# Merging key blocks in a bank, a whole bias table with reversed queries, short last units and a hand-placed job table in a fused attention and expert layer

## The reference

```python
x = x + attn(layernorm(x))
#   Q, K, V = silu(x @ Wq), silu(x @ Wk), silu(x @ Wv);  U = x @ Wu
#   scores = (Q K^T + rel_bias[i - j + 255]) / sqrt(16), NEG where j > i or K's row is all zero
#   attn = (silu(scores) @ V) * silu(U)          (silu, not softmax)
x = x + ffn(layernorm(x))
#   logits = x @ w_gate.T; top 2 of 8, softmax over the two; y = sum_e gate_e * (x @ w_in[e].T) @ w_out[e].T
```

## Time and profile before

| what | value |
|---|---|
| median of 3 runs | 362.77 us (362.26 to 366.17) |
| profiled execution, its time | 364.07 us |
| its span | 360.8 us |
| mean granted TensorE clock | 0.92 |
| TensorE matmuls busy | 318.1 us |
| VectorE busy | 256.8 us |
| ScalarE busy | 235.4 us |
| GpSimd busy | 142.3 us |
| DMA, mean | 101 GB/s |

### The profile page before, as it was taken

The page is one execution under the profiler, slowest core; times in us unless marked ns, Lnnn a source line. Parts: engine busy times, 40 slices in busy tenths (PEclk is TensorE's granted clock), DMA queues, the critical chain, the costliest instruction groups (busy, mean ns, idle before and its releaser), DMA issues.

```text
span 360.8 us, 5741 instructions
## 1 busy us (share of the span) xinstructions
PE 318.1 (88%) x1728; PEld 137.7 (38%) x1728; DVE 256.8 (71%) x773; ACT 235.4 (65%) x485; POOL 142.3 (39%) x205
## 2 busy tenths in 40 slices
PE   4699975999999899899988999999999989998392
PEld 3442422555343343234323444443334423423240
DVE  3545671747749958676768978878789597786586
ACT  2345883889974776587745786788757885774022
POOL 3541120102108660138156551085286313654446
PEclk9998995999999987699989987999999998999678
DMA  6618968124924930005914940028449200010001
GB/s 207 174 48 208 194 179 247 58 60 121 236 54 146 224 70 2 1 8 171 214 16 143 221 105 0 0 70 224 89 144 222 73 2 0 1 31 1 0 9 49
DMA packets 30685, 36.31 MB, mean 101 GB/s; under 512 B 3256, under 2 KB 17080, under 8 KB 30656
## 3 DMA queue, kind: packets, MB, share of 16 engines
q1 hardware_dynamic: 30080, 35.69, 39.9%
q10 hardware_dynamic: 576, 0.26, 0.3%
HBM read 23.87 MB, written 12.08 MB: 100 GB/s over the span
## 4 chain that ended last, share of the span: by engine, by line
PE 50%; DVE 25%; ACT 9%; DMA 8%; issue 5%; SPq 2%; POOL 0%; DVEq 0%
PE jobp L637 12%; PE o_acc L568 12%; PE score L555 8%; DVE score L809 8%; ACT wts L696 7%; PE jobp L599 4%; DMA rows_dram<-k_hi 3%; DVE xn L853 3%; DVE ymix L922 3%; PE jobp L630 3%; PE jobp L657 2%; DMA rows_dram<-q_lo 2%; PE jobp L592 2%; DVE stats L840 2%; DMA ymix<-in_L_ffn_w_out 2%
## 5 line engine op out<-in xcount | busy, mean ns | idle before, releaser
L696 ACT ACTIVATE wts<-score,far 128x512 f32<-128x512 f32 (+3 forms) x384 | 193.4, 589 | 69.7 <-DVE score L809 57.9
L809 DVE TENSOR_TENSOR score<-score,bias_near 128x384 f32<-128x384 f32 (+2 forms) x320 | 119.0, 436 | 33.4 <-PE score L555 33.0
L507 POOL TENSOR_TENSOR ymix<-ymix 128x512 f32<-128x512 f32 (+2 forms) x84 | 69.4, 826 | 82.3 <-DVE ymix L922 77.9
L555 PE MATMUL score<-q_stack,k_stack 64*128 64x512 f32 (+3 forms) x352 | 82.1, 426 | 10.1 <-ACT wts L696 4.5
L568 PE MATMUL o_acc<-wts,v_pad 128*32 128x512 f32 (+3 forms) x768 | 86.8, 525 | 2.3 <-DVE oT L821 1.4
L555 PEld LDWEIGHTS score<-q_stack,k_stack 64*128 64x128 f32 x352 | 39.9, 193 | 74.9 <-issue 47.5
L637 PE MATMUL jobp<-mm_e,xn2T 128*128 128x512 f32 x116 | 65.5, 669 | 0.0
L922 DVE TENSOR_TENSOR ymix<-jobp,gates 128x512 f32<-128x512 f32 x56 | 38.0, 686 | 20.4 <-PE jobp L637 19.6
L637 PEld LDWEIGHTS jobp<-mm_e,xn2T 128*128 128x128 f32 x116 | 20.0, 201 | 31.9 <-issue 27.7
L455 POOL TENSOR_TENSOR rstd<-mv,eps_t 128x4 f32<-128x4 f32 x16 | 3.2, 201 | 69.3 <-DVE mv L843 69.3
L568 PEld LDWEIGHTS o_acc<-wts,v_pad 128*32 128x32 f32 x768 | 15.4, 109 | 26.5 <-issue 18.7
(11 more groups left out here) (92 smaller groups left out, 272.3 us busy)
## 6 DMA issues: line engine op xcount, KB each, us to landing
k_stack<-rows_dram SPq DMA_DIRECT2D x32, 256.0 KB, 5.7
q_stack<-rows_dram SPq DMA_DIRECT2D x28, 256.0 KB, 6.4
rows_dram<-k_hi SPq DMA_DIRECT2D x16, 256.0 KB
xs<-in_L_attn_x SPq DMA_DIRECT2D x8, 256.0 KB, 7.9
rows_dram<-k_lo SPq DMA_DIRECT2D x8, 256.0 KB
rows_dram<-q_hi SPq DMA_DIRECT2D x7, 256.0 KB
rows_dram<-q_lo SPq DMA_DIRECT2D x7, 256.0 KB
out<-xs SPq DMA_DIRECT2D x7, 256.0 KB, 2.3
```

The costliest lines, as they stand in the source:

```text
L507: then_wait(pool.tensor_tensor(y[:, 0:n], y[:, 0:n], y[:, n:2 * n], ALU.add))
L555: pe.matmul(score[bank][:, 0:n], keys, queries, start=True, stop=True).then_inc(scored[bank], 1)
L696: act.activation(wts[:, number % 2, j, 0:n], score[bank][:, 0:n], ACT.Silu, bias=far[:, h:h + 1], scale=HD ** -0.5).then_inc(weighed[bank], 1)
L809: dve.tensor_tensor(scores, scores, bias_near[:, 4 * quad + j, c0:c0 + near], ALU.add)\
```

## The change

- **Units and groups.** `UNITS` replaces the halves. The last half of the last batch becomes two units of two tiles. In a unit of four tiles the diagonal blocks of 384 and 128 queries form one group of 512 columns in one bank; in a unit of two tiles two key blocks of 256 queries do. A half 0 has 3 groups a quad, a half 1 has 7, the last units 3 and 4: 20 a batch, 80 in all. Each block is still its own score matmul, bias addition and P·V product; one activation covers the bank. There are 320 activations instead of 384.
- **Bias.** Queries lie reversed within a half: the Q product reads its rows backwards, and the gating reads `o_acc` backwards. The transfers from `bias_dram` then write the final table, and flip, FLIP jobs and their copies go. The table has 512 columns of whole bias (the first 128 filled with the far value by GpSimd). Groups that lie within it add all their columns and use no far value; others use `bias_rel` (the difference to far, made on GpSimd by `REL`: two subtractions of 1024 columns) and the far value as before.
- **Jobs.** `plan_timeline` goes; the table of slots is written out, with up to three banked jobs in a slot. Three slots precede group 0. T1, Q and K of half 1 of batch 0 stand beside groups 1 and 2, K of half 0 is split directly, and experts 1 and above follow from slot 6 on.
- **Norms.** All except norm1 of batch 0 and norm2 of the last unit run on GpSimd, behind their reciprocal root: 14 normalisations, 54 tiles.
- **Top 2.** An 8-wide maximum sorts a tile's logits; comparisons with its second entry choose, and gates take two operations.
- **Loads.** Expert 1 is loaded behind the write of `bias_dram`; experts 4 to 7 are issued from ScalarE's queue behind the `M` of the expert they replace. Rows of q and k of half 1 are written together. `kpad` lies in the place of batch 3's x.
- **End.** SEL to FF of two tiles only. Their four FF products wait in four score banks, and `MIX` adds expert by expert from PSUM on VectorE, two tiles in turn. The last two stores go from two queues.

```diff
+UNITS = [(b, HT * half, HT) for b in range(B - 1) for half in range(2)] + [(B - 1, 0, HT), (B - 1, HT, 2), (B - 1, HT + 2, 2)]
...
+def part(u, kb):
+    b, f, tiles = UNITS[u]
+    return u, kb, P * (f + tiles - max(kb, f)), P * (f + tiles - kb)
+def steps(u):
+    b, f, tiles = UNITS[u]
+    last = f + tiles - 1
+    if tiles == HT:
+        blocks = [(kb,) for kb in range(last - 2)] + [(last - 2, last), (last - 1,)]
+    else:
+        blocks = [(kb, kb + 1) for kb in range(0, last, 2)]
+    return [(quad, [part(u, kb) for kb in kbs]) for quad in range(QUADS) for kbs in blocks]
...
-GROUPS = [[(kb, max(kb * P, half * HALF), (half + 1) * HALF - max(kb * P, half * HALF)) for kb in range((half + 1) * HT)]
-          for half in range(2)]
...
+def all_near(group):
+    return all(total <= BANK for u, kb, n, total, c in parts_of(group)[1])
+def some_near(group):
+    return any(total - n < NEAR for u, kb, n, total, c in parts_of(group)[1])
...
+def norm_on_dve(job):
+    return job[:2] == ("norm1", 0) or job == ("norm2", LAST)
...
+BEFORE = [
+    [("stats1", 0, 0), ("RB",), ("WT", 0)],
+    [("norm1", 0, 0), ("M", 0), ("stats1", 0, 1)],
+    [("T1", 0, 0), ("K", 0, 0), ("Q", 0, 0), ("split", 0, 0), ("norm1", 0, 1)],
+]
+BESIDE = [
+    [("V", 0, 0), ("MASK", 0, 0)],
+    [("T1", 0, 1), ("Q", 0, 1), ("REL",)],
+    [("K", 0, 1), ("split", 0, 1), ("U", 0, 0), ("V", 0, 1)],
+    [("MASK", 0, 1)],
+    [],
+    [("stats1", 1, 0), ("U", 0, 1)],
+    [("norm1", 1, 0), ("WT", 1), ("stats1", 1, 1)],
+    [("SEL", 0), ("stats2", 0), ("norm1", 1, 1), ("M", 1), ("WT", 2)],
+    [("T1", 1, 0), ("norm2", 0), ("M", 2)],
+    [("K", 1, 0), ("Q", 1, 0), ("split", 1, 0)],
+    [("T1", 1, 1), ("T2", 0)],
...
+    [("FF", 0, 2, 0), ("FF", 0, 2, 1), ("SEL", 1), ("stats2", 1)],
+    [("norm2", 1), ("Q", 2, 0), ("U", 1, 1)],
+    [("T2", 1), ("V", 2, 0), ("MASK", 2, 0)],
+    [("FF", 0, 3, 0), ("FF", 0, 3, 1)],
...
+AFTER = [
+    [("FF", 3, 2, 0), ("FF", 3, 2, 1), ("FF", 3, 3, 0), ("FF", 3, 3, 1), ("best", 7, 1), ("tanh", 7),
+     ("gates", 7), ("FF", 3, 4, 0), ("FF", 3, 4, 1), ("FF", 3, 5, 0), ("FF", 3, 5, 1)],
+    [("SEL", 8)],
+    [("stats2", 8), ("norm2", 8)],
+    [("T2", 8)],
+    [("LOG", 8)],
+    [("FF", 3, 6, 0), ("FF", 3, 7, 0), ("FF", 3, 6, 1), ("FF", 3, 7, 1)],
+    [("best", 8, 0)],
+    [("best", 8, 1), ("tanh", 8)],
+    [("gates", 8)],
+    [("MIX",)],
+]
...
+            sp.wait_ge(ext_set, 2)
             wait_drained(sp, ("RB",))
             sp.dma_start(bias_dram, ext[:]).then_inc(ext_out, 16)
+            load_expert(1)
             sp.wait_ge(ext_out, 16)
             for quad in range(QUADS):
...
+                sp.dma_start(bias_near[:, 4 * quad:4 * quad + 4, BANK - NEAR:BANK],
+                             bass.AP(bias_dram.tensor, quad * BANK, [[1, P], [2 * BANK, 4], [1, NEAR]]))\
                     .then_inc(bias_in[quad], 16)
             write_rows(0, 0, 1)
-            write_rows(0, 1, 0)
             load_x(1, 0)
             load_stack(0, 0, 1)
+            write_rows(0, 1, 0)
+            write_rows(0, 1, 1)
             load_stack(0, 1, 0)
-            write_rows(0, 1, 1)
+            load_stack(0, 1, 1)
             load_x(1, 1)
...
+                if not norm_on_dve((("norm1", "norm2")[ln],) + args):
+                    pool.wait_ge(scaled, n + 1)
+                    normalise(pool, args, ln)
...
+                for u, kb, n, total, c in parts:
+                    half, q0 = first_column(u)
+                    if u == 0:
+                        keys, queries = kpad[rows32, quad, kb * P:(kb + 1) * P], qk32[0][rows32, q0:q0 + n]
+                    else:
+                        keys = k_stack[rows64, b % 2, head, kb * P:(kb + 1) * P]
+                        queries = q_stack[rows64, half, head, q0:q0 + n]
+                    ins = pe.matmul(score[bank][:, c:c + n], keys, queries, start=True, stop=True)
+                ins.then_inc(scored[bank], 1)
...
+                for i, (u, kb, n, total, c) in enumerate(parts):
+                    half, q0 = first_column(u)
+                    for j in range(4):
+                        ins = pe.matmul(o_acc[32 * j:32 * j + 32, q0:q0 + n], v_pad[:, b % 2, kb, 4 * quad + j, :],
+                                        wts[:, group % WTS, j, c:c + n], start=USES["o", u][0] == group and i == 0,
+                                        stop=USES["o", u][-1] == group and i == len(parts) - 1)
...
+                    rows = xn1T[:, half * HALF:(half + 1) * HALF]
+                    ins = pe.matmul(bank[:], w[:], rows[:, ::-1] if kind == "Q" else rows, start=True, stop=True)
...
-                elif kind == "FLIP":
-                    i = args[0]
-                    pe.wait_ge(bias_in[i // 3], 16)
-                    pe.wait_ge(flip_set, 1)
-                    ins = pe.matmul(bank[:], flip[:], bias_rev[:, i * BANK:(i + 1) * BANK], start=True, stop=True)
...
+                    if e + 4 < E:
+                        wout_e, win_e = expert_in(e + 4)
+                        act.dma_start(wout_e, w_out[e + 4]).then_inc(wout_in[e % 4], 16)
+                        act.dma_start(win_e, w_in[e + 4].rearrange("(c p) d -> p c d", p=P)).then_inc(win_in[e % 4], 16)
...
+                if all_near(group):
+                    act.activation(weights, score[bank][:, 0:n], ACT.Silu, scale=HD ** -0.5).then_inc(weighed[bank], 1)
+                else:
+                    act.activation(weights, score[bank][:, 0:n], ACT.Silu, bias=far[:, h:h + 1], scale=HD ** -0.5)\
+                        .then_inc(weighed[bank], 1)
...
+                for u, kb, n, total, c in parts:
+                    if all_near(group):
+                        near, bias = 0, bias_near[:, 4 * quad + j, BANK - total:BANK - total + n]
+                    else:
+                        near = total - NEAR
+                        bias = bias_rel[:, 4 * quad + j, 0:n - near]
+                    ins = dve.tensor_tensor(score[bank][:, c + near:c + n], score[bank][:, c + near:c + n], bias, ALU.add)
+                ins.then_inc(biased[bank], 1)
...
+                dve.tensor_tensor(oT[:, cols], o_acc[:, q0:q0 + P * tiles][:, ::-1], uT[:, b % 2, cols], ALU.mult)\
+                    .then_inc(gated, 1)
...
+                        ins = dve.scalar_tensor_tensor(xs[:, B - 1, t], bank_of(job)[:, c:c + D], gates[:, t, e:e + 1],
+                                                       xs[:, B - 1, t], ALU.mult, ALU.add)
...
+                    for t in tiles:
+                        ins = dve.max(top[:, 0, t], lg[:, 0, t])
+                    then_wait(ins)
+                    for t in tiles:
+                        dve.scalar_tensor_tensor(lg[:, 1, t], lg[:, 0, t], top[:, 0, t, 1:2], rank[:], ALU.is_ge, ALU.mult)
+                    dve.tensor_tensor(gap[:, ts], top[:, 0, ts, 0], top[:, 0, ts, 1], ALU.subtract).then_inc(top_ready, 1)
+                    then_wait(dve.tensor_tensor(lg[:, 2, ts], lg[:, 0, ts], wide(top[:, 0, ts, 1]), ALU.is_gt))
+                    dve.tensor_tensor(pick[:, 1, ts], lg[:, 0, ts], wide(top[:, 0, ts, 0]), ALU.is_equal)
+                    then_wait(dve.scalar_tensor_tensor(lg[:, 1, ts], lg[:, 2, ts], 2.0 * E, lg[:, 1, ts], ALU.mult, ALU.add))
+                else:
+                    for t in tiles:
+                        ins = dve.max(top[:, 1, t], lg[:, 1, t])
+                    then_wait(ins)
+                    then_wait(dve.tensor_tensor(pick[:, 0, ts], lg[:, 1, ts], wide(top[:, 1, ts, 1]), ALU.is_ge))
...
+                then_wait(dve.scalar_tensor_tensor(pick[:, 1, ts], pick[:, 1, ts], -0.5,
+                                                   half_tanh[:, ts].unsqueeze(2).to_broadcast([P, n, E]), ALU.add, ALU.mult))
+                dve.scalar_tensor_tensor(gates[:, ts], pick[:, 1, ts], 0.5, pick[:, 0, ts], ALU.add, ALU.mult)\
+                    .then_inc(gates_ready, 1)
```

692 lines of the change are left out of this document (310 added, 382 removed), and 17 rows, old and new, of the table BESIDE.

## The result

The changed kernel takes 389.49 us (median of 4 runs, 383.80 to 390.39) where the kernel before, on the same chip, takes 364.34: ratio 1.060, interval 1.043 to 1.078. It is slower, where 327 us were forecast. The profiled execution has a span of 388.2 us and took 390.39.

The account below looks back on a forecast made before the run. No engine bounds it throughout: start and tail are latency chains, batches 1 to 3 a hand-over loop paid per group. Gains of 13 (start), 20 (batches 1 to 3) and 3 (tail) sum to 36 us: 327 us, range 308 to 345.

Parts of the forecast that it names:

- The cover is its idle time: Batches 1 to 3: GpSimd, busy 106 of 222 us, absorbs 19 us of normalisations in its idle time.
- Rival (d): GpSimd's norms come late, TensorE stops at transpositions, 4.9 us each; all fourteen give 396 us; chance 0.04 for slower.
- GpSimd's tile: Normalising one tile on GpSimd takes 0.46 us, like its 128x128 addition; upper end 0.83.
- The collision: VectorE and GpSimd delay each other; normalisations leave VectorE, selection may now meet them: gain and loss set equal.
- The start: Up to batch 0's end: scores at 15.5 us, unit 1 ending at 95.5 instead of 108.4, 13 us gained; bounds 5, 19.
- their split ends near 27: Start: half 1's T1, Q, K wait for ScalarE's turn in groups; split near 27 us, q stack at 38.
- Batches 1 to 3: Fewer, wider groups save ScalarE 10.6 us busy and 9.7 idle, sum 20 us; bounds 5 and 33.
- it is paid per weighing, not per column: Batches 1 to 3: ScalarE's idle time before weighings is 0.81 us a group; twelve fewer save 9.7.
- rival (b): Batches 1 to 3 keep their pace, ScalarE's idle time being per column; only start and tail gain: 345 us; chance 0.16.
- VectorE's busy time: Batches 1 to 3: net 10 to 16 us less, 163 of 202 us, 81% busy against 79%.
- The tail: After the last P·V: 27 us against 29.9, 3 us gained, GpSimd's sums standing ahead of the last rstd.
- Rival (c): Denser groups end TensorE's stops and keep its clock up: 13 us of clock more, 309 us; chance 0.17.

Follow-up runs that it names:

- e2: Changed kernel with T2 of units 1 to 7 one slot later: 364.18 us, ratio 1.003.
- e9: Kernel before with its norms on GpSimd and T2 one slot behind the norm in six of eight halves, three slots from statistics: 350.72 us, ratio 0.968.
- e13: Kernel before with its norms on GpSimd and only two slots from statistics to T2: 382.56 us, ratio 1.048.
- e1: Changed kernel with all norms back on VectorE: 375.96 us, ratio 1.034.
- e3: Changed kernel with T1, K, Q and split of half 1 of batch 0 in a slot ahead of the first group: 375.10 us, ratio 1.032.
- e7: Changed kernel with late T2, early half 1 and the last unit's chain ahead of independent feed-forward products: 344.78 us, ratio 0.963.
- e11: e7 with the merged groups split again, 14 groups more: 353.92 us, ratio 0.979.
- e12: e7 with every bias addition of VectorE covering only 8 columns: 321.92 us, ratio 0.886.
- e8: e7 with all norms on VectorE: 350.42 us, ratio 0.978.
- the best version: e7, the changed kernel with late T2, early half 1 and reordered tail: 344.78 us, ratio 0.963.
- e4: Kernel before with the same norms moved to GpSimd and its table left alone: 362.08 us, ratio 0.989.
- e15: e13 run once more for its trace: 379.59 us, one time.
- e5: Changed kernel with both late T2 (e2) and early half 1 (e3): 350.23 us, ratio 0.976.
- e16: e7 run once more to look at its first gating: 342.64 us, one time.

## Why the prediction was wrong

**The distance was never counted.** This is the step that failed, and it turned the sign: "The cover is its idle time". With it the sum holds nothing for the "about six such places" where norm and transposition stand close. Rival (d) named the mechanism, with a chance of 0.04, against which stood "GpSimd is idle half of the stage". That says nothing on a chain that starts only when its input is there. The stage shows eight stops, 27.9 us idle, and the same stage of the kernel before none; with `T2` a slot later 4.1 us are left (`e2`).

The working that was at hand: statistics 1.3, power and sum 1.3, four tiles at a price between 0.46 and 0.83, together 4.4 to 5.9 us, against two slots of some 3.7 us (`e2`: 219.3 us for 60 groups), of which little is left when TensorE reaches `T2` as early as 0.3 to 3.5 us behind the start of the statistics. The slots from `stats2` to `T2` stand in both tables, 4 to 6 and 2. The prediction spoke only of "a slot or two" between norm and transposition (2 or 3 before, 1 after); `e9` and `e13` indicate that with GpSimd's norms the slots count from the statistics.

The price of a stop, 4.9 us in (d), came out near by luck. The stage's clock was short by 0.11 x 242.4 = 26.7 us where the earlier trace rows give 0.06 x 222.5 = 13.4, and (27.9 + 13.3) / 8 = 5.2 us a stop. But these are 3.5 us of idle time and 1.7 of clock, where 1.5 and 3.4 were set.

**GpSimd's tile** was taken at 0.46 us and measured 0.79 to 0.81. The upper bound (0.83) held. The value was that of a 128x128 addition, nearest in shape and not in kind. At 0.46 the chain would be 1.3 us shorter, as an estimate at most 10.6 of the 27.9 us; `e1`, with the quicker engine, still has 17.9. The Trainium skill ("GPSIMD Engine Reference", Engine selection) would have one-input work on GpSimd near line rate; this trace disagrees, with a median of 0.80 us against VectorE's 0.34.

**The collision** of VectorE and GpSimd that the prediction weighed as even came out small, in batches 1 to 3: a cast of k went from 815 to 417 ns, while four operations of the new selection took 302 to 414 ns where others of their size take 184 to 192.

**The start** was forecast to gain 13 us and lost 8.6. The table and the first scores are there at 18.8 us instead of 15.5. The failed step is "their split ends near 27": it rests on groups of 3 to 3.5 us, with nothing set for the jobs of half 1 that "now run inside unit 0". The groups took 4.3 us with TensorE busy all the time. T1, Q and K of half 1 wait in slots beside groups 1 and 2, the split is done at 42.3. Rows and q stack then take 16.1 us where 11 were set: the load leaves at 49.5, the stack is there at 58.4, and TensorE stands 14.0 us. With half 1 ahead of the first group (`e3`) batch 0 ends at 100.8 us, a gain of 7.6 of the forecast 13; unit 0 still occupies TensorE until 46. The lower bound was a gain of 5 with a q stack at 48.

**Batches 1 to 3** were to gain 20 us. With the stops gone they gain 3.2 (`e2`) to 6.3 (`e7`). The busy half of the term came true and more: weighings cost 128.5 us where 138.2 were forecast, since those without the far value take some 90 ns less (598 instead of 690 at 512 columns), and four lie outside the window. The idle half did not: 64.1 us in `e7` for 236 weighings, 0.27 each, instead of 0.21 of 283. The failed step is "it is paid per weighing, not per column", read from four equal means: `e11` with 40 more weighings has 61.5 us of it. Most of it ends with an addition of VectorE, and it shrinks when these are light (`e12`); that it goes by what stands in VectorE's queue fits this, but why the four means were equal is not shown. This was rival (b), given 0.16, and with the stops gone it is what the batches did.

VectorE's busy time was forecast right (163 us, measured 163.4 to 164.5), in part by luck: bias additions grew by 13.2 us where 9 were set, and casts fell by 3.7, which no term held. It fits in the stage but comes late.

**The tail** was right in its path: 28.8 us against 27, the last root behind GpSimd's sums at 374.74 us, 15.3 behind the last gating (forecast 14.2), against the earlier trace rows one microsecond gained instead of three. `MIX` takes 5.2 us with its hand-overs (380.99 to 386.22) where 4.3 were set.

**Clock.** Rival (c) fell: without stops the clock is 0.93 to 0.94, as in the earlier trace rows; in `e8` it is 0.97, and the three batches take 217.9 us all the same.

**What the best version gains** against the profiled span before, 360.8 - 342.5 = 18.3 us: 7.6 until batch 0 ends, 6.3 in batches 1 to 3, 4.4 in the tail. The kernel before with GpSimd's norms three slots behind the statistics is quicker in batches 1 to 3 (`e9`: 211.8 us against 216.2), so the written table is not the best one there. Why its planner's order gains 7 us when transpositions come earlier (`e4` to `e9`, 218.4 to 211.8 us) wasn't examined.

## What to carry to other kernels

Where an in-order engine consumes what other engines make, write down for each such job the chain of durations from its last input to its output and the slots of the table that it has, before and after the change. A free engine does not shorten a chain. An equal mean wait for all shapes does not show that the wait is paid per instruction: ask whose queue it ends in.

## What was not expected of the hardware

- A normalisation (two per-partition scalars) of a 128x128 tile cost GpSimd 784 to 834 ns in `e9` and VectorE 324 ns at least and 335 in the median. Single ones took longer in other traces, up to 1.3 us on either engine.
- One slot of distance was worth 32 us in a kernel of 350 (`e9`, `e13`). Of the 25.7 us between the spans of the two traces (`e9`, `e15`) 22.5 are TensorE's wait for normalised tiles.
- Two kernels that differ only in the tail had a granted clock of 0.50 and 1.00 in the same 8 us near the start (`e5`, `e16`), TensorE busy in both.
- An activation with a bias column takes 690 ns at 512 columns, one without 598.
